# Sine and cosine of the recurrence's angles by polynomials on GpSimd, the Gelu table loaded first, and the first weight splits in another order

## What is computed

```
xn = layernorm(x)
nu = softplus(nu_log); mag = exp(-exp(nu)); theta = exp(theta_log)     # 32 states
A_re = mag * cos(theta); A_im = mag * sin(theta); gamma = sqrt(1 - mag*mag)
Bu_re, Bu_im = xn @ (gamma * B_re).T, xn @ (gamma * B_im).T
h_re[t] = A_re*h_re[t-1] - A_im*h_im[t-1] + Bu_re[t]
h_im[t] = A_re*h_im[t-1] + A_im*h_re[t-1] + Bu_im[t]
s = h_re @ C_re.T - h_im @ C_im.T + D * xn
g = silu(gelu(xn @ proj1.T + proj1_bias) @ proj2.T + proj2_bias)
x = x + s * g
```

## Time and profile before

| what | value |
|---|---|
| median of 3 runs | 824.03 us (823.12 to 824.19) |
| span of the profiled execution | 821.5 us |
| PE busy | 803.2 us, 98% |
| DVE busy | 667.3 us, 81% |
| ACT busy | 522.1 us, 64% |
| POOL busy | 466.3 us, 57% |
| mean granted clock of PE | 0.998 |

### The profile page before, as it was taken

One profiled execution on the slowest core, in us unless ns is written; L12 is line 12 of the kernel. 1 busy time (PEld: TensorE's weight loads), 2 busy tenths in 40 slices (PEclk: granted clock), 3 DMA queues, 4 the chain that ended last, 5 costly groups with the idle time before them and its releaser, 6 DMA issues.

```text
span 821.5 us, 24195 instructions
## 1 busy us (share of the span) xinstructions
PE 803.2 (98%) x8552; PEld 760.6 (93%) x8552; DVE 667.3 (81%) x2509; ACT 522.1 (64%) x1612; POOL 466.3 (57%) x1245
## 2 busy tenths in 40 slices
PE   7999999999999999999999999999999999999988
PEld 5988999888889899999999999999999999999977
DVE  6898786888687888878788897878888878887875
ACT  5555454445645786775767677677766767677572
POOL 6823112203226776676757667666676756667653
PEclk9999999999999999999999999999999999999999
DMA  8510011000002223222232212223222232212210
GB/s 306 227 34 1 1 66 65 1 1 1 1 14 45 45 47 57 49 49 40 45 54 50 53 34 46 45 50 56 41 51 37 45 55 44 60 34 48 42 41 28
DMA packets 101338, 41.22 MB, mean 50 GB/s; under 512 B 91745, under 2 KB 98401, under 8 KB 100577
## 3 DMA queue, kind: packets, MB, share of 16 engines
q1 hardware_dynamic: 98896, 38.89, 20.4%
q10 hardware_dynamic: 2320, 0.79, 0.4%
HBM read 14.47 MB, written 4.19 MB: 23 GB/s over the span
## 4 chain that ended last, share of the span: by engine, by line
PE 89%; DVE 4%; issue 2%; ACT 2%; POOL 2%; DMA 1%; ACTq 0%; POOLq 0%; DVEq 0%
PE bank L492 59%; PE bank L684 17%; PE bank L706 9%; PE bank L556 1%; POOL par L1723 1%; PE bank L566 1%; PE bank L606 1%; PE bank L509 1%; DVE QA L1490 1%; DVE PT L1524 1%; ACT SM L973 1%; DVE SM L1502 1%; PE bank L580 0%; DMA QT<-QA 0%; PE bank L631 0%
## 5 line engine op out<-in xcount | busy, mean ns | idle before, releaser
L1884 POOL TENSOR_SCALAR SM<-SM,stb 128x32 f32<-128x32 f32 (+7 forms) x512 | 194.7, 398 | 100.2 <-DVE stb L1509 96.7
L973 ACT ACTIVATE SM<-SM,stb 128x32 f32<-128x32 f32 (+7 forms) x512 | 206.1, 404 | 61.7 <-DVE stb L1502 58.0
L684 PE MATMUL bank<-KT,QT 128*128 128x192 f32 (+7 forms) x1024 | 166.9, 306 | 5.0 <-DVE stb L1502 4.8
L684 PEld LDWEIGHTS bank<-KT,QT 128*128 128x128 f32 x1024 | 146.9, 190 | 9.2 <-DVE stb L1502 5.9
L1502 DVE CUSTOM_DVE_ANT_0 SM<-bank,CONST 128x32 f32<-128x32 f32 (+7 forms) x512 | 126.6, 298 | 35.2 <-PE bank L684 32.2
L492 PE MATMUL bank<-yh,wq_lo 128*128 128x256 f32 x512 | 148.2, 289 | 0.2 <-DVE QA L1490 0.2
L492 PE MATMUL bank<-yl,wq_hi 128*128 128x256 f32 x512 | 144.1, 281 | 0.0
L492 PE MATMUL bank<-yh,wq_hi 128*128 128x256 f32 x512 | 144.0, 281 | 0.0
L1524 DVE STREAM_TRANSPOSE PT<-SM 128x384 f32<-128x384 f32 (+3 forms) x256 | 115.6, 480 | 22.9 <-PE bank L706 22.9
L492 PEld LDWEIGHTS bank<-yh,wq_lo 128*128 128x128 f32 x512 | 96.6, 189 | 0.4 <-DVE QA L1490 0.4
L492 PEld LDWEIGHTS bank<-yl,wq_hi 128*128 128x128 f32 x512 | 96.6, 189 | 0.0
(11 more groups left out here) (207 smaller groups left out, 1986.1 us busy)
## 6 DMA issues: line engine op xcount, KB each, us to landing
QT<-QA SPq DMA_DIRECT2D x248, 64.0 KB, 2.2
C<-KV SPq DMA_DIRECT2D x256, 16.0 KB, 1.8
out<-fo SPq DMA_DIRECT2D x32, 128.0 KB, 2.0
X<-in_x SPq DMA_DIRECT2D x7, 512.0 KB, 10.9
stage<-in_wqn SPq DMA_DIRECT2D x2, 1024.0 KB, 9.6
stage<-in_wo SPq DMA_DIRECT2D x2, 1024.0 KB, 5.1
stage<-in_w1t SPq DMA_DIRECT2D x4, 256.0 KB, 5.3
stage<-in_w2t SPq DMA_DIRECT2D x2, 512.0 KB, 6.9
```

Source lines behind the costliest of these rows:

```text
L684: i = e.matmul(sbank[n % 2][:, at], Q[:, p, q, :, :].rearrange("p h c -> p (h c)"), KT[b % 3][:, p, 0:32 * q + 32], start=True, stop=True)
L973: i = e.activation(M[:, at], M[:, at], ACT.Exp, bias=S[:, 0, j:j + 1], scale=-1.0, accum_out=S[:, 1, j:j + 1])
L1884: i = e.tensor_scalar(P[:, at], P[:, at], S[:, 2, j:j + 1], 1.0, ALU.mult, ALU.mult)
```

## The change

Three things are changed.

1. POOL computes sine and cosine of the 8 reduced angles itself. Half the angle is squared, and sine over x and cosine of the half angle are polynomials in the square with seven coefficients each, side by side in 16 columns, summed in pairs (`ODD`, `EVEN`, `SUMS`, `PAIRS` in a new tile `trig`); the sine and cosine of the whole angle follow from those of the half. That is 15 instructions in place of 9 and L1781, and 14 memsets of coefficients at the start. ACT's `angles()` and the semaphores `ang` and `sin` are gone.
2. ACT's first instruction is a Gelu of one column in place of a Sin of one, so Gelu's table is the one that is loaded first.
3. On ACT, `w2_high(0)` goes from step 1 to step 0, `w2_high(2)` from 3 to 4, `w1_high(3)` from 0 to 3. On DVE, `w2_low(0)` goes from step 1 to 0 and `w2_low(2)` from 3 to 4, `w1_low(3)` from 0 to 3; the norm of chunk 1, which is issued in pieces, starts at step 1 and not 0, with 5 pieces a step and not 4.

The diff, without the edits of the semaphore table:

```diff
@@ -229,6 +230,7 @@
         rs0 = sb("rs0", [128, 5, 4], F32, l0)
         ri0 = sb("ri0", [128, 4], I32, l0)
         VEC0 = sb("VEC0", [128, OFF_BB], F32, l0)
+        trig = sb("trig", [128, 16, 16], F32, l0)
         l0.close()
 
         l1 = ExitStack()
@@ -871,11 +873,6 @@
                 w.wait_ge("bt", 16)
                 e.activation(bh[:, :, :], bts, ACT.Copy).then_inc(SEM["bh"], 1)
 
-            def angles():
-                w.wait_ge("ang", 1)
-                w.wait_ge("sin", 1)
-                e.activation(col(48, 16), col(32, 16), ACT.Sin).then_inc(SEM["sin"], 1)
-
             def m_high():
                 w.wait_ge("wm", 80)
                 e.activation(LB[0][:, :], lbs, ACT.Copy).then_inc(SEM["lbh"], 1)
@@ -1014,7 +1011,7 @@
             e.dma_start(X[:, 0:2, :].rearrange("p a b -> p (a b)"), x[:, 0:2 * D]).then_inc(SEM["x0"], 16)
 
             w.wait_ge("par", 1)
-            e.activation(col(56), tsn[:, 0:1], ACT.Sin).then_inc(SEM["sin"], 1)
+            e.activation(trig[:, 15, 0:1], tsn[:, 0:1], ACT.Gelu)
             w1_high(0)
             x_high(0, 0)
             x_high(0, 1)
@@ -1037,19 +1034,17 @@
                     w1_high(1)
                 if g == 0:
                     w1_high(2)
-                if g == 0:
+                if g == 3:
                     w1_high(3)
                 if g == 65:
                     mids(0, wbank)
                 if g == 55:
                     y_high(0, wbank)
                 if g == 0:
-                    angles()
-                if g == 1:
                     w2_high(0)
                 if g == 2:
                     w2_high(1)
-                if g == 3:
+                if g == 4:
                     w2_high(2)
                 if g == 5:
                     w2_high(3)
@@ -1562,11 +1557,9 @@
                 if g == 48:
                     l1_norm(0)
                     l1_norm(1)
-                if g == 1:
-                    w2_low(0)
                 if g == 2:
                     w2_low(1)
-                if g == 3:
+                if g == 4:
                     w2_low(2)
                 if g == 6:
                     w2_low(3)
@@ -1583,6 +1576,8 @@
                 if g == 0:
                     w1_low(2)
                 if g == 0:
+                    w2_low(0)
+                if g == 3:
                     w1_low(3)
                 if g in (9, 12, 20, 28, 36, 44, 52, 60):
                     c = (9, 12, 20, 28, 36, 44, 52, 60).index(g)
@@ -1607,9 +1602,9 @@
                 c, r = divmod(g - 11, 8)
                 if r == 0 and 0 <= c < NC:
                     l0_gate(c, 1)
-                if g == 0:
+                if g == 1:
                     norm = l0_norm(1)
-                go(norm, 4)
+                go(norm, 5)
                 if g == 65:
                     turn_queries(0, 0)
                 if g == 66:
@@ -1764,6 +1759,15 @@
             done[0] += 1
 
 
+            ODD, EVEN, SUMS, PAIRS = (trig[:, i:i + n, :] for i, n in ((0, 3), (3, 3), (6, 4), (10, 2)))
+            q1, q2, q4 = (trig[:, i, :] for i in (12, 13, 14))
+            for k in range(7):
+                at = SUMS[:, 3, :] if k == 6 else (ODD if k % 2 else EVEN)[:, k // 2, :]
+                e.memset(at[:, 0:8], float((-1) ** k / math.factorial(2 * k + 1)))
+                i = e.memset(at[:, 8:16], float((-1) ** k / math.factorial(2 * k)))
+            i.then_inc(SEM["par"], 1)
+            done[0] += 1
+
             w.wait_ge("nuth", 16)
             exact_exp(col(1), col(3), None)
             turns(col(24), col(3))
@@ -1777,22 +1781,26 @@
                 ts(v8, ab, part, None, ALU.mult)
                 tt(r8, r8, v8, ALU.subtract)
             ts(r8, r8, PI, -PI, ALU.min, ALU.max)
-            w.wait_ge("par", done[0])
-            e.tensor_scalar(ab, r8, 0.5, None, ALU.mult, ALU.bypass).then_inc(SEM["ang"], 1)
             exact_exp(col(0), col(2), "nu")
 
 
-            s8, c8, w8, v8 = col(48, 8), col(56, 8), col(32, 8), col(40, 8)
-            w.wait_ge("sin", 2)
-            tt(c8, c8, c8, ALU.mult)
-            ts(c8, c8, -2.0, 1.0, ALU.mult, ALU.add)
-            tt(w8, s8, s8, ALU.mult, free=True)
-            tt(v8, c8, c8, ALU.mult)
-            tt(w8, w8, v8, ALU.add)
-            ts(w8, w8, -0.5, 1.5, ALU.mult, ALU.add)
-            tt(s8, s8, w8, ALU.mult)
-            tt(c8, c8, w8, ALU.mult, free=True)
-            ts(v8, s8, -1.0, 1.0, ALU.mult, ALU.mult)
+            s8, c8, v8 = col(48, 8), col(56, 8), col(40, 8)
+            ts(ab, r8, 0.5, None, ALU.mult)
+            both = ab.unsqueeze(1).broadcast_to([128, 2, 8])
+            tt(q1.rearrange("p (i n) -> p i n", i=2), both, both, ALU.mult)
+            tt(SUMS[:, 0:3, :], ODD, q1.unsqueeze(1).broadcast_to([128, 3, 16]), ALU.mult)
+            tt(q2, q1, q1, ALU.mult, free=True)
+            tt(SUMS[:, 0:3, :], SUMS[:, 0:3, :], EVEN, ALU.add)
+            tt(q4, q2, q2, ALU.mult, free=True)
+            tt(PAIRS, SUMS[:, 1:4:2, :], q2.unsqueeze(1).broadcast_to([128, 2, 16]), ALU.mult)
+            tt(PAIRS, PAIRS, SUMS[:, 0:3:2, :], ALU.add)
+            tt(q1, PAIRS[:, 1, :], q4, ALU.mult)
+            tt(q1, q1, PAIRS[:, 0, :], ALU.add)
+            tt(r8, r8, q1[:, 0:8], ALU.mult)
+            tt(s8, r8, q1[:, 8:16], ALU.mult)
+            tt(c8, r8, r8, ALU.mult, free=True)
+            ts(c8, c8, -0.5, 1.0, ALU.mult, ALU.add)
+            ts(v8, s8, -1.0, 1.0, ALU.mult, ALU.mult, free=True)
             for i in range(8):
                 n = 2 ** i
                 ts(g1[:, 0:n], tsn[:, 0:n], col(40 + i), 1.0, ALU.mult, ALU.mult)
```

More of the change, by code:

```diff
@@ L1 @@
+import math
 from contextlib import ExitStack
@@ L70 @@
     "mx", "r", "qa", "pt", "otl", "ob",
-    "clean", "par", "ang", "nu", "tab", "rt", "fill", "rl", "lr", "kr", "kvr", "n", "qq", "nw", "rs", "oc", "kwk", "kwv",
+    "clean", "par", "nu", "tab", "rt", "fill", "rl", "lr", "kr", "kvr", "n", "qq", "nw", "rs", "oc", "kwk", "kwv",
 )
```

2 lines of the change are left out of this document (1 added, 1 removed).

## The result

The changed kernel takes 825.70 us (median of 7 runs, 823.33 to 827.01). The kernel before took 823.12 us in the runs beside it (median of 7, 822.46 to 824.19). The ratio is 1.0027, with a 95% interval of 1.0017 to 1.0038: **slower by 0.27%, 2.2 us**; the two medians lie 2.6 us apart. The forecast was 825.4 us, within 822.6 to 827.0. The level was hit better than the difference: the forecast meant +1.4 us beside the 824.03 us of before, and +2.6 us beside 823.12 us is what came.

The account below looks back on a forecast made before the run. PE was taken to bound nearly all, with POOL's tables holding scan(0). scan(0) 0.3 us later plus 1.1 us of lost clock gave 1.4 us on the median of 824.03: 825.4 us, range 822.6 to 827.0.

Parts of the forecast that it names:

- The bound: Whole kernel: PE bounds nearly all of it, so what the first 62 us give or cost arrives whole at the end.
- The front: First Gelu: 2.61 us stall and 1.4 us of half clock go; of 4.0 us PE keeps about 3.4.
- POOL's chain: POOL's tables before scan(0): new piece 6.7 us in place of 5.64, tables at 41.6, scan(0) 0.3 us later.
- the price of 0.47 us for a DVE instruction: POOL's 15 instructions: each of five DVE instructions alongside costs POOL 0.47 us, 2.4 us in all.
- The bounds: Tables at 40.0 with 0.2 us per DVE instruction, at 42.9 with 0.68; scan(0) moves by -1.3 to +1.6 us.
- 0.4 was said: POOL's tables, late part: hl(8) on DVE now falls ahead of their end and costs another 0.4 us.
- Z and the clock: PE's first product with Z: waits over 4 us, half clock behind it, no slack left; 1.1 us later, bounds 0 and 1.6.
- The 0.3 us that I took off: Half clock at Z: 1.1 us taken in place of 1.4, because the stretch's start may already lie in the wait.
- The sum: End of kernel: 0.3 us for scan(0) plus 1.1 us for the clock, 1.4 us later, 825.4 us.
- idle of 1.2 us and less was harmless: PE's clock: argument for the rival that it holds behind the wait for Z, +0.3 us, 824.3 us, chance 0.17.

Follow-up runs that it names:

- the first experiment: Changed kernel with POOL's second exponential left out and replaced by one instruction, so magnitudes are wrong: 820.52 us, ratio 0.9966.
- the second profile: Changed kernel run and profiled once more, without any edit: median 826.08 us, ratio 1.0029; the profiled execution took 823.20 us.
- the first profile: Profiled execution of the changed kernel in its first 7 runs, the fastest of them: 823.33 us, span 821.5 us.
- the version with the exponential on ACT: Changed kernel with POOL's RR scaling behind tsi and the polynomial of nu's exponential on ACT, only its reduction on POOL: 821.66 us, ratio 0.9989.
- the two with filler: Changed kernel with useless PE products before the wait for Z: 11 products 825.37 us, ratio 1.0025; 6 products 823.92 us, ratio 1.0012.
- operations of one input: Changed kernel with low parts of w1's fourth and w2's third quarter written as zeros by one-input DVE operations: 824.85 us, ratio 1.0015.
- that with RR behind: Changed kernel with POOL's scaling of RR behind tsi, scan(0) waiting for tci and tsi only: 824.02 us, ratio 1.0010.
- the old order: Changed kernel with the weight splits and the norm of chunk 1 back in the order of before: 823.70 us, ratio 1.0008.
- the last version: Changed kernel with RR behind tsi, the polynomial of nu's exponential on ACT, and tci made by ACT at step 9: 821.37 us, ratio 0.9977.
- the kernel before with RR moved: Kernel before with RR's scaling behind tsi on POOL, the scan waiting for two tables, the product with Z for three: 822.49 us, ratio 0.9999.
- the kernel before in the new order: Kernel before with only the third part of the change, the new order of splits and norm: 823.70 us, ratio 1.0010.

## Why the prediction came out as it did

**The bound.** Right, by the first experiment. But "whatever the first 62 us give or cost arrives at the end whole" is not: in the second profile layer 0 ends 2.25 us later than in the first, and the spans are 821.4 and 821.5. Behind 246 us DVE waits for a transfer on its way to the queries (QT), and there 1.0 us of the lateness goes:

```profile
257.80 2.48 DVE L1485 TENSOR_TENSOR QA<-bank,TR 128x512 f32<-128x512 f32 x4 [3.73 <-DMA QT<-QA]
```

```profile
259.03 2.49 DVE L1485 TENSOR_TENSOR QA<-bank,TR 128x512 f32<-128x512 f32 x4 [2.72 <-DMA QT<-QA]
```

The first row is the first profile, the second row the second. The other 1.2 us go in steps of 0.3, 0.5 and 0.5 us at three waits of DVE in layer 1, ahead of a transpose (L1519, PT): 1.68, 1.82 and 1.82 us in the first profile near 410, 551 and 622 us, 1.44, 1.34 and 1.34 in the second. These waits differ from execution to execution, late or not: in the version with the exponential on ACT, which is early, they are 1.26, 1.46 and 1.27 us, in the kernel before 1.68, 1.82 and 1.62. So 1.0 us is slack that takes up lateness, and the rest looks like the second profile's luck in layer 1; why these waits differ is not shown. The profiled executions are at the fast end of their kernels' runs (823.33 and 823.2 of medians of 825.70 and 826.08), so how much the usual run gets back is not known.

**The front.** The stall and the half clock went, as said. hl(1) starts at 18.75 (18.8 was said), and PE waits 1.05 us for it in place of the 0.5 that I said; 0.17 us of that is a wait of the statistics for their load. A second wait, 0.55 us for xl at 30.72, was not in the sum at all. So PE comes to Z 2.3 us earlier than before and not 3.5 (at 42.6 in place of 41.4), and that is why its wait there is 2.9 to 3.7 us and not over 4. It costs nothing, since PE waits for Z anyway.

**POOL's chain.** The second exponential ends at 20.56 (the range was 19.7 to 20.3). The 15 instructions take 5.68 us, 5.97 in the second profile, where 6.7 was said: the price of 0.47 us for a DVE instruction was too high. Undisturbed 4.3 us leave 1.4 to 1.7 for five, some 0.3 each, since POOL's short instructions got about one turn for each DVE instruction. The prediction counted the new piece against one in which a POOL instruction had been held for two DVE instructions at once (1.43 us) and took that for the rule. It was one draw of a lottery that runs from 0.3 us each to 3.10 for all. The bounds were also added up wrongly: by the prediction's own terms the tables come at 40.12 - 0.34 + 0.4 = 40.2 with 0.2 us per DVE instruction and at 40.12 + 2.06 + 0.4 = 42.6 with 0.68, not at 40.0 and 42.9. What saved the sum, by luck, is that the doubling rounds behind were longer than I said: from the first G to tsi's end 15.3 us, 15.6 in the second profile, against 14.8 before; 0.4 was said, 0.5 and 0.8 came. The tables end at 41.49 and 42.23; 41.6 was said. Of four more profiles with this chain, the two with filler have tsi's end at 42.23 and 42.31, that with operations of one input at 41.95, and that with RR behind at 41.67, which with RR's 0.48 us is 42.15. So 42.2 is nearer to the usual place, and this step was short by 0.6 us.

**Z and the clock.** Mechanism and place are those of the second profile: half clock behind a wait of 3.7 us ("over 4" was said), no slack at states_out, everything passed on to the turn. The size was short by 0.4 us: 1.55 us in place of 1.1. The 0.3 us that I took off because the stretch may start inside the wait did not apply: it starts 0.3 us behind the wait's end, and all of its 3.4 us fall on work.

**The sum.** Said: 0.3 + 1.1 = 1.4. By the second profile: 0.9 for scan(0) and 1.5 for the clock, 2.4 us at the turn; measured 2.6 us by the medians. That the two agree proves little, since the execution of the second profile did not itself end late. Both terms had the right sign and were mis-sized the same way. The median came within 0.3 us of the forecast by luck: the kernel before took 0.9 us less in these runs than in those shown.

**What stays open.** What makes the clock fall. It fell behind waits of PE of 2.61 us (the kernel before, inside the wait) and 3.70 us (the second profile), 1.1 us behind the end of one of 2.79 us (the old order), and at PE's first products behind 1.14 us (the last version, and the kernel before with RR moved). It held behind 2.86 us (the first profile), 3.18 (the kernel before in the new order), 3.31 (the changed kernel with RR moved) and 3.70 us (operations with one input). The same wait of 3.70 us did both, so the length of the wait does not decide it, and a short wait is no protection; the prediction's "idle of 1.2 us and less was harmless" is true of the one trace it was read from. That the wait for Z is what makes low clocks frequent in the changed kernel rests on the counts (10 of 19, and none of 22 with filler) and on one profile; against it stands that the kernel with RR moved has 1 of 12 with a wait of 3.31 us. Also, of a run without a profile only the mean clock is known; that a second and a third stretch lies elsewhere (in two profiles of other versions one lies at 261 and at 279 us, in layer 1) follows from the mean, not where it lies in the changed kernel's slowest runs.

## What to carry to other kernels

A stall taken away at the front is worth only what the next bound leaves of it; look up what the next meeting of the chains waits for, and if it has 1.3 us of slack, and the change makes it later besides, 3 to 4 us of gain become a longer wait there, and then also ask what that wait does to PE's clock and how much slack is behind it. A wait of PE like these (2.6 to 3.7 us) does least harm where the engines behind it have slack; where they have none, independent work in the wait can pay, even useless work, as long as it ends before the wait does (six products paid here, eleven did not). Small chains on POOL are better not laid beside rows of large DVE instructions on SBUF: part of such a chain can go to ACT if that waits anyway, as in the last two versions. And a profile is one execution: here two of the same kernel lie 2.2 us apart at the turn, nearly the whole effect, and none in the span.
